# Unread full-array turns of the identity in front of some of TensorE's waits, in three narrow attentions of a decoder

## The reference

```python
# L1_attn: masked self-attention of 256 rows
mask = (j % 32 == 0) | (abs(i - j) <= 64)
scores = einsum('bhid,bhjd->bhij', q, k) * dh ** -0.5
attn = softmax(where(mask, scores, -inf))
return (attn @ v) @ w_out + b_out

# L3_xattn: two attentions in a row
h = _mha(x, x, x, ..., causal=True)            # 256 keys, lower triangle
out = _mha(h, ctx, ctx, ..., causal=False)     # 1601 keys of the context
```

## Time and profile before

| what | value |
|---|---|
| median of 3 runs | 3913.87 us |
| the three runs | 3901.09, 3913.87, 3919.18 us |
| profiled execution, its own time | 3946.06 us |
| its span, first to last instruction | 3944.3 us |
| TensorE busy, share of the span | 84% |
| VectorE, ScalarE, GpSimd busy | 66%, 49%, 32% |
| mean granted clock of TensorE | 0.892 |
| first masked attention | about 477 to 612 us of the span |
| second masked attention | about 3290 to 3440 us |
| context attention | about 3442 to 3869 us |

### The profile page before, as it was taken

One profiled execution on the slowest core, in us unless ns is written; L12 is line 12 of the kernel. 1 busy time (PEld: TensorE's weight loads), 2 busy tenths in 40 slices (PEclk: granted clock), 3 DMA queues, 4 the chain that ended last, 5 costly groups with the idle time before them and its releaser, 6 DMA issues. The chain is left out here.

```text
span 3944.3 us, 96221 instructions
## 1 busy us (share of the span) xinstructions
PE 3325.7 (84%) x40498; PEld 2328.4 (59%) x40498; DVE 2616.4 (66%) x4510; ACT 1952.2 (49%) x3525; POOL 1267.1 (32%) x842
## 2 busy tenths in 40 slices
PE   7566697999999998766649668999999988999996
PEld 4445665777777776731123345666666665667774
DVE  5124385666666666379977777888888864567773
ACT  1122344655555554359961234566665652345553
POOL 1101303555555553410021236655666631000000
PEclk9577888999999999788868889999999996789997
DMA  1021501000000000810000211111111101000000
GB/s 40 6 63 50 166 1 39 1 10 1 10 1 1 1 1 8 257 58 1 1 5 1 60 58 44 48 54 42 51 52 42 26 21 40 9 19 20 11 2 11
DMA packets 88726, 131.40 MB, mean 33 GB/s; under 512 B 18450, under 2 KB 60106, under 8 KB 87532
## 3 DMA queue, kind: packets, MB, share of 16 engines
q1 hardware_dynamic: 85292, 119.03, 10.6%
q0 software_dynamic: 3008, 6.23, 0.4%
HBM read 86.63 MB, written 10.94 MB: 25 GB/s over the span
## 5 line engine op out<-in xcount | busy, mean ns | idle before, releaser
L2786 POOL TENSOR_TENSOR wide_probs<-wide_probs,wide_factor 128x1024 f32<-128x1024 f32 x128 | 239.6, 1893 | 311.1 <-ACT wide_factor L2747 311.1
L2743 ACT ACTIVATE wide_probs<-wide_ps_s,wide_nm 128x1024 f32<-128x1024 f32 (+1 forms) x256 | 237.2, 927 | 172.6 <-DVE wide_nm L2828 152.8
L175 POOL TENSOR_TENSOR model_Y<-model_Y,model_X 128x512 f32<-128x512 f32 x12 | 15.2, 1268 | 942.4 <-POOLq L66 942.4
L2294 ACT ACTIVATE narrow_probsT<-narrow_ps 128x512 f32<-128x512 f32 (+1 forms) x448 | 220.1, 582 | 136.0 <-PE narrow_ps L2198 133.6
L2823 DVE TENSOR_REDUCE wide_nm<-wide_ps_s 128x1 f32<-128x1024 f32 x128 | 156.0, 1219 | 193.6 <-PE wide_ps_s L2629 193.6
L2348 DVE TENSOR_REDUCE narrow_part<-narrow_ps 128x1 f32<-128x512 f32 x384 | 242.4, 685 | 52.6 <-PE narrow_ps L2181 50.2
L3933 POOL TENSOR_TENSOR local_turn<-local_turn 128x1024 f32<-128x1024 f32 x96 | 226.7, 2369 | 157.0 <-DVE local_turn L3991 156.8
L3147 DVE TENSOR_TENSOR bonds_strain<-peri_in_moved 128x1664 f32<-128x1664 f32 (+3 forms) x128 | 257.0, 2085 | 1.0 <-PEq L66 1.0
L3198 PE MATMUL bonds_ps<-bonds_act_of,bonds_out 128*32 128x448 f32 (+3 forms) x1024 | 153.5, 697 | 117.9 <-ACT bonds_act_of L3171 83.9
L2181 PE MATMUL narrow_ps<-second_KQ 32*128 32x512 f32 x768 | 247.2, 668 | 1.1 <-ACT second_KQ L2265 1.0
L2641 PE MATMUL wide_ps<-model_ident,wide_probs 128*128 128x128 f32 (+1 forms) x1664 | 238.9, 274 | 10.8 <-DVE wide_probsT L2833 9.1
(11 more groups left out here) (643 smaller groups left out, 8452.0 us busy)
## 6 DMA issues: line engine op xcount, KB each, us to landing
moe_w<-in_L_ffn_w SPq DMA_DIRECT2D x62, 512.0 KB
local_V<-local_V SPq DMA_DIRECT2D x96, 128.0 KB
e_wqkv<-in_L_ffn_qkv SPq DMA_DIRECT2D x6, 1536.0 KB, 7.2
local_V<-local_V SPq DMA_DIRECT2D x144, 64.0 KB
context_rows<-in_ctx SPq DMA_DIRECT2D x8, 768.0 KB
e_keys<-in_ctx_T SPq DMA_DIRECT2D x6, 800.5 KB, 4.9
e_source<-in_ctx_T SPq DMA_DIRECT2D x4, 800.5 KB, 4.4
second_source<-in_ctx_T SPq DMA_DIRECT2D x4, 800.5 KB, 5.7
```

The costliest lines, as they stand in the source:

```text
L2294: act.activation(probsT[0:high, c % PROBS, h, 0:wide], bank[0:high, 0:wide], ACT.Exp).then_inc(t_taken_act.sem, 1)
L2743: act.activation(probs[:, n % 2, h, lo:hi], ps_s[h][:, 0:hi - lo], ACT.Exp, bias=nm[:, n % 2, h, 2 * half:2 * half + 1], scale=1.0, accum_ ...
L2786: pool.tensor_tensor(v, v, factor[:, n // 4 % 2, j:j + 1].broadcast_to([P, CUT]), ALU.mult).then_inc(lowered[i].sem, 1)
```

## The change

`warm(bank, many)` puts `many` transposes of the identity by the identity into columns 0 to 127 of the bank that TensorE has just taken for the unit. Nobody reads them; the unit's own matmuls overwrite them. Each is a weight load of 128 x 128 and a matmul of 128 columns on all 128 rows.

In both masked attentions they stand before the wait for the data of `lift` (3), `divide` (3), `gather` (4) and `final` (4). For that the wait for the bank, which stood behind the data's wait, is moved ahead of it. In the context attention 6 stand behind the bank's wait of every fourth score unit of step 0 alone, 7 times. The two masked attentions get 16 x 3 + 16 x 3 + 4 x 4 + 4 x 4 = 128 turns each and the context attention 42, in all 298. No unit is moved in the plan, and no other engine's instructions change.

```diff
--- before.py
+++ after.py
@@ -2118,6 +2118,10 @@
         def _(pe):
             pe.wait_ge(loaded.sem, loaded.nth(LOADS))
 
+            def warm(bank, many):
+                for _ in range(many):
+                    pe.transpose(bank[:, 0:P], m.ident[:, :], m.ident[:, :])
+
             for e in plan:
                 kind, s, n = e
                 b, g = s // G, s % G
@@ -2168,6 +2172,8 @@
                             side, nth = taken_t(("query", 0, 1))
                             pe.wait_ge(side.sem, side.nth(nth))
                     bank, made = empty(pe, e)
+                    if a.context and s == 0 and n % 4 == 0:
+                        warm(bank, 6)
                     Kh, Qh = KQ_of(s)[part_of(h), 0:K], KQ_of(s)[part_of(h), K:]
                     if t is None:
                         at = 0
@@ -2181,8 +2187,10 @@
                         mm = pe.matmul(bank[:, 0:hi - lo], Qh[:, t * P:(t + 1) * P], Kh[:, lo:hi], start=True, stop=True)
                     mm.then_inc(made.sem, 1)
                 elif kind == "lift":
+                    bank, made = empty(pe, e)
+                    if a.masked:
+                        warm(bank, 3)
                     pe.wait_ge(top_ready.sem, top_ready.nth(s + 1))
-                    bank, made = empty(pe, e)
                     for t in range(TB):
                         mm = pe.transpose(bank[:, t * P:(t + 1) * P], top[:, s % 2, t, :], m.ident[:, :])
                     mm.then_inc(made.sem, 1)
@@ -2223,20 +2231,26 @@
                         at += q1 - q0
                     mm.then_inc(pv_made.sem, 1)
                 elif kind == "divide":
+                    bank, made = empty(pe, e)
+                    if a.masked:
+                        warm(bank, 3)
                     pe.wait_ge(pv_taken.sem, pv_taken.nth(s + 1))
-                    bank, made = empty(pe, e)
                     for t in range(TB):
                         mm = pe.transpose(bank[:, t * P:(t + 1) * P], OTx[:, t * P:(t + 1) * P], m.ident[:, :])
                     mm.then_inc(made.sem, 1)
                 elif kind == "gather":
+                    bank, made = empty(pe, e)
+                    if a.masked:
+                        warm(bank, 4)
                     pe.wait_ge(s_taken.sem, s_taken.nth(s_rank["divide", s, 0] + 1))
-                    bank, made = empty(pe, e)
                     for t in range(TB):
                         mm = pe.transpose(bank[:, t * P:(t + 1) * P], O[:, b % 2, t, :], m.ident[:, :])
                     mm.then_inc(made.sem, 1)
                 elif kind == "final":
+                    bank, made = empty(pe, e)
+                    if a.masked:
+                        warm(bank, 4)
                     pe.wait_ge(s_taken.sem, s_taken.nth(s_rank["gather", s, 0] + 1))
-                    bank, made = empty(pe, e)
                     if a.columns:
                         mm = pe.matmul(bank[:, 0:T], wo[:, :], OT[:, :], start=True, stop=True)
                     else:
```

## The result

The change takes 3895.3 us (median of 9 runs, 3888.76 to 3906.18), the kernel before beside it 3912.56 us (9 runs, 3901.09 to 3931.39): ratio 0.9959, 95% interval 0.994 to 0.9979. That is 17 us less, less than 0.5%, with an interval that leaves no change out. The profiled execution took 3898.96 us, its span 3897.2 us, 47 us less than the span before.

The account below looks back on a forecast made before the run. TensorE was taken to set the pace at the low clock, VectorE at the high one. Gains of 53 us less 8 paid took the profile's 3946.06 us to 3901; the range went from some 5 us below 3869 up to 3922.

Parts of the forecast that it names:

- The profiled execution was the unlucky one: Whole kernel: timed runs mostly had the high clock in the long stretch already; lands at 3901 us, chance 0.43.
- the long slow stretch: Second masked attention, 3305 to 3380 us: seven steps in 75 us at clock 0.50, expected to take 41 to 42.
- The case of 3869 us: Rival, whole kernel: the slow stretches are in every run, so the whole 45 us show; chance 0.38.
- Unread transposes hold the clock: Masked attentions and context step 0: turns raise the clock, so can hold it; rival not held, 3934 us, chance 0.14.
- the Trainium skill's rule on transposes: TensorE's clock: the high clock does not engage for transposes; by it the change would buy nothing, time 3934 us.
- Second masked attention 33 us: Second masked attention, 3305 to 3380 us: gain of 33 us from full clock, bounded by 38.
- First 9: First masked attention, 492 to 523 us: 22 us expected at full clock, a gain of 9, bound 14.
- Tail and context attention 3 + 8: Second masked attention's tail gains 3 us, bound 5; the context attention's step 0 gains 8, bound 11.
- the term that the prediction put at 6 us: Masked attentions' steps at full clock: turns cost 0.3 us a step in the first, 0.15 in the second, 13 each.
- at the high one VectorE does: Masked attentions at clock 1.00: VectorE sets the pace, working 59.04 of 64 us and 29.87 of 32.
- 0.33 us fits into 0.62: Lift at full clock: its turns fit between TensorE's end at 3399.42 and VectorE taking the result at 3400.04.
- 8 paid: Whole kernel: turns cost 6 us in steps, 1 in gathers and finals, 1.2 in the context; 8 in all.

Follow-up runs that it names:

- order_only: The change with all its turns taken out and only the moved waits for the bank kept; ratio 0.9992 to the kernel before.
- ctx_only: The change with only the context attention's 42 turns, those of the masked attentions taken out; ratio 0.9972 to the kernel before.
- tail_only: The change with turns only at divides from step 12 and gather and final of step 15 of both masked attentions; ratio 0.9959 to the kernel before.
- dve_extra: The kernel before with one unread 128 x 512 addition on VectorE in each step of the masked attentions; one run, 3924.34 us.
- double: The change with 6, 6, 8 and 8 turns in the masked attentions and none in the context attention; one run, 3914.13 us.
- ends: The change with masked turns only at lifts of steps 0 to 2, divides from step 12, last gather and final; context turns kept; ratio 0.9937 to the kernel before.
- start_only: The change with turns only at the lifts of steps 0 to 2 of both masked attentions; 3884.22 us, ratio 0.9912 to the kernel before.
- thin: The change in the masked attentions alone, each turn replaced by an unread matmul of 64 columns on 32 rows; one run, 4005.24 us.

## Why the prediction was right

It said 3901 us in a range of 3864 to 3922, and that the ratio would be within 0.5%. 3895.3 us came. The mechanism was right, the two sizes in it were both too small, and that they cancel is luck.

**The profiled execution was the unlucky one: right.** Of the 86 timed runs of the kernel before, seven lie at 3939 to 3949 us and the next at 3931. Five traces have no turns at the first lifts (before, order_only, ctx_only, tail_only, dve_extra), and the long slow stretch is in one of them. That the runs near 3940 are those with the long stretch is inferred, since none of them has a trace. The case of 3869 us fell with this: a fixed addition of the profile would also be in the change's own profile, which lies 4 us above its median.

**Unread transposes hold the clock: right.** The first masked attention lost the clock at its start in all five of those traces, and in none of the seven with full-array turns at the first lifts. That the Trainium skill's rule on transposes ("TensorE: Matmul & The Clock Gate", Part 4: PE-mode transpose) does not hold here, for float32 transposes, is thus shown by runs as well.

**The gains, by stretch.** Second masked attention 33 us predicted; 116.9 - 84.3 = 32.6. First 9; 105.0 - 93.6 = 11 at least. Tail and context attention 3 + 8 = 11; against the profile before (58.2 - 49.8) + (373.5 - 365.5) = 16. Together some 60 for 53. But the context's 8 us are those of one execution: the other seven traces without its turns have 366.7 or 366.9 there, 1.2 us above the change.

**The cost: wrong in size.** This is the term that the prediction put at 6 us for the steps at full clock, 0.3 and 0.15 us a step. Measured: 0.66 in both, 92.2 - 84.3 = 7.9 us in the second attention and 100.1 - 93.6 = 6.5 at least in the first, 14 us for the 7 that the steps, gathers and finals were put at. Steps of 7.12 and 6.01 us are the sign that the prediction itself had named as wrong (longer by 0.6 us). The step that failed is "at the high one VectorE does" set the pace, and with it "0.33 us fits into 0.62". It compared when the lift's result was ready with when VectorE took it. That is the slack of one result. TensorE goes through `plan` in order, and what it makes next is late by every turn; double shows that nothing of it is taken up, and dve_extra that the spare time was VectorE's. The hint was in the earlier trace rows: TensorE in flight 97% and VectorE 92 to 93%. (A smaller slip: the digit of the earlier trace rows at 480 us is an 8, and the 7s lie before 394 us.)

The two errors, 7 us of gain too little and 7 of cost too little, cancel in the profile's account: 45 us predicted, 653.6 - 607.6 = 46 measured in the four columns. The span's 47 has luck of its own: between the two masked attentions the changed kernel's trace is 10 us longer, and behind the context attention 10 us shorter, and the change touches neither.

**What the timed runs gained.** Mostly not the long stretch, which is in few of them. The clock of the kernel before is 0.890 to 0.909 in its timed runs, that of the change 0.910 to 0.914 in all 20 of its own. By the line, 0.900 to 0.911 is worth some 36 us, and the change lies 20 us and more above the line. So the timed runs, too, gained nearly twice the 21 us that the forecast leaves them (3914 to 3901, and 8 paid), and paid over twice the 8. This is an estimate from the line. Where in the program they gained is not shown: the start of the first masked attention (105.0 to 100.1 with its turns paid) and the tail (49.8 and 48.2 for 51.6 or more) are shorter in each trace of the change than in each without its masked turns, and for the rest there is no such row. The few runs near 3940 are gone as well (the change's highest in 20 runs is 3906), but 7 in 86 is too seldom for 20 runs to show it.

That the middle turns are a loss is shown by ends: middle steps of 6.46 us again, the clock held all the same, and 8 us above the line for the change's 21 to 23. Its ratio is lower too, 0.9937 for 0.9959, though the two intervals overlap.

## What to carry to other kernels

Unread full-array work bought clock here where a stretch used few rows of the array, and cost its full length where TensorE had no spare time; it belongs at the thin start and the thin tail of a stage, not in every step. The 18 turns of start_only gave the lowest ratio of all, 0.9912, not to be told from that of ends. To find an engine's slack, don't look at how long one of its results lies waiting: add a known piece of work to it and see how much of it the step grows. A profile with one long slow stretch may be a rare execution; compare its own time with the timed runs before its microseconds are promised. Where every timed run has its mean clock, set time against clock: it parts what a change buys from what it costs, which the medians alone don't.

## What the runs showed of the hardware

TensorE's granted clock fell from 1.00 to 0.50 with the engine in flight for 4.00 of 4.00 us, 21 of 27 matmuls on 32 rows (thin), and held in the same places with three 128-row transposes in front of each lift. Transposes alone raised it from 0.50 to 1.00 (TensorE had nothing in flight for 12.56 us before them). An unread turn costs 0.11 us a piece at full clock, also right behind 32-row matmuls; an fp32 matmul of 64 columns on 32 rows cost 0.16 to 0.21 us there ((7.44 - 6.46) / 6 and (6.60 - 5.35) / 6, thin). In the kernel before, 0.001 of mean granted clock is worth 3.2 us of 3910 (77 timed runs).
